# Four graph layers: the node work of layers 1, 2 and 4 is done in units of 512 nodes inside the gather passes

## The reference, cut to what matters

```python
x = _layernorm(x + GAT(x))        # 4 heads; softmax over the edges of a node; skip product; its own layer norm
x = _layernorm(x + GCN(x))        # linear, batch norm over all nodes, leaky relu, product, sum over edges, log_softmax
x = _layernorm(x + HGT(x))        # 8 heads; keys and values gathered, queries by target; product, skip, norm, elu
x = _layernorm(x + SchNet(x))     # filters from 50 edge features; sum over edges; lin2, softplus, lin
```

## Time and profile before

| what | value |
|---|---|
| runs | 9010.18 us median of 3 (9009.75 to 9013.16) |
| profiled execution | 9027.8 us, of it the span from first to last instruction 9025.8 us |
| busy | PE 5296.0, PEld 4295.5, DVE 4797.4, ACT 1743.0, POOL 6159.4 us |
| mean granted TensorE clock | 0.663 of full speed |

### The profile page before, as it was taken

How to read it: one execution, slowest core, us unless ns; L and a number is a source line. 1 busy time by engine, 2 the same in 40 slices (tenths; PEclk the granted TensorE clock), 3 DMA queues, 4 the chain that set the end, 5 groups by cost and what they waited for, 6 DMA issues and landing times. The chain is left out here.

```text
span 9025.8 us, 88124 instructions
## 1 busy us (share of the span) xinstructions
PE 5296.0 (59%) x27493; PEld 4295.5 (48%) x27493; DVE 4797.4 (53%) x10730; ACT 1743.0 (19%) x2681; POOL 6159.4 (68%) x6485
## 2 busy tenths in 40 slices
PE   4555555553244444444456666666656888887884
PEld 3454444443233333333335555555544555555553
DVE  5666666666522222222257777777775555555554
ACT  0000000001200000000030000000016555555553
POOL 5777777771177777777637777777745777777772
PEclk6666665666555555555577777777767788788786
DMA  5444333431133333333245555555522222222221
GB/s 175 112 116 112 112 111 113 115 112 26 31 79 75 75 77 75 76 76 77 60 126 163 164 164 165 163 165 162 165 85 69 73 74 74 73 73 73 74 73 34
DMA packets 391525, 906.28 MB, mean 100 GB/s; under 512 B 134486, under 2 KB 202897, under 8 KB 368209
## 3 DMA queue, kind: packets, MB, share of 16 engines
q0 software_dynamic: 232704, 538.22, 23.3%
q1 hardware_dynamic: 153458, 351.32, 12.9%
q10 hardware_dynamic: 4896, 11.01, 0.3%
HBM read 867.62 MB, written 32.45 MB: 100 GB/s over the span
## 5 line engine op out<-in xcount | busy, mean ns | idle before, releaser
L1647 POOL DMA_INDIRECT PM<-hgt_kv_table,src_idx x1616 | 1532.5, 948 | 655.7 <-issue 468.3
L634 POOL DMA_INDIRECT PM<-gat_table,src_idx x1616 | 1536.2, 951 | 546.1 <-issue 492.2
L2217 POOL DMA_INDIRECT TMP<-schnet_table,src_idx x1616 | 1538.7, 952 | 541.0 <-issue 490.0
L1178 POOL DMA_INDIRECT PM<-gcn_table,src_idx x1004 | 952.4, 949 | 306.1 <-issue 304.3
L1178 POOL DMA_INDIRECT TMP<-gcn_table,src_idx x612 | 578.9, 946 | 550.7 <-POOLq L1038 364.4
L1206 PE MATMUL ps<-TMP,PM 128*128 128x128 f32 x2008 | 516.0, 438 | 704.8 <-DMA PM<-gcn_table,src_idx 704.8
L1253 DVE TENSOR_TENSOR AC<-AC,ps 128x128 f32 x101 | 29.2, 289 | 1526.4 <-PE ps L1206 1526.4
L679 PE MATMUL ps<-PM 128*128 128x139 f32 x3232 | 779.7, 433 | 66.7 <-DVE PM L773 66.4
L1206 PEld LDWEIGHTS ps<-TMP,PM 128*128 128x128 f32 x2008 | 444.3, 326 | 766.1 <-DMA PM<-gcn_table,src_idx 627.9
L679 PEld LDWEIGHTS ps<-PM 128*128 128x128 f32 x3232 | 738.6, 326 | 73.1 <-DVE PM L773 72.7
L2244 PE MATMUL ps<-PM 128*128 128x128 f32 x3232 | 551.2, 325 | 335.4 <-issue 210.7
(11 more groups left out here) (386 smaller groups left out, 8790.3 us busy)
## 6 DMA issues: line engine op xcount, KB each, us to landing
PM<-local_dst_row SPq DMA_DIRECT2D x101, 1024.0 KB
PM<-local_dst_row SPq DMA_DIRECT2D x202, 512.0 KB, 3.9
PM<-in_attrT SPq DMA_DIRECT2D x101, 400.0 KB
xT<-in_rel_row SPq DMA_DIRECT2D x101, 384.0 KB, 4.7
PM<-gat_table,src_idx POOLq DMA_INDIRECT x1616
PM<-hgt_kv_table,src_idx POOLq DMA_INDIRECT x1616, 3.1
TMP<-schnet_table,src_idx POOLq DMA_INDIRECT x1616, 2.5
PM<-gcn_table,src_idx POOLq DMA_INDIRECT x1004, 2.5
```

The lines of the kernel that those rows point to most:

```text
L634: pool.indirect_dma_start(out=g[:, par, t, 0:TAB0], out_offset=None, in_=tab0_d, in_offset=bass.IndirectOffsetOnAxis(ap=src_idx[:, i * ROU ...
L1178: pool.indirect_dma_start(out=g[n % DEEP][:, k, :], out_offset=None, in_=tab1_d, in_offset=bass.IndirectOffsetOnAxis(ap=src_idx[:, n * KT ...
L1647: pool.indirect_dma_start(out=g[:, par, t, 0:2 * P], out_offset=None, in_=kv_d, in_offset=bass.IndirectOffsetOnAxis(ap=src_idx[:, i * ROUN ...
L2217: pool.indirect_dma_start(out=g[:, b, k, :], out_offset=None, in_=tab3_d, in_offset=bass.IndirectOffsetOnAxis(ap=src_idx[:, (i * SLOTS + b ...
```

## The change

Nodes are cut into 13 units of 512 (the last has 2 tiles of 128 instead of 4). The node work of layers 1, 2 and 4 is cut into stages (9, 8 and 8), and a unit takes one stage in each round, beginning at a round by which its nodes can get no more edges. The schedule is fixed when the program is built:

```diff
+PACE, LAG = 62, 60
+                s.link(dve.scalar_tensor_tensor(span, iota_f[:, 0:NR], -float(PACE), bounds[:, 0:NR], ALU.mult, ALU.add))
+                s.link(dve.tensor_reduce(ahead, span, AX.X, ALU.min))
+                s.link(dve.scalar_tensor_tensor(nar, ahead, -float(LAG), nar, ALU.is_ge, ALU.mult))
...
+        def first_round(u):
+            r = -(-(KT * P * (u + 1) + LAG) // PACE) + 1
+            return r if r < NR else None
+        def due(i, stages):
+            return [(u, i - first_round(u)) for u in range(GROUPS4) if first_round(u) is not None and 0 <= i - first_round(u) < stages]
+        def left_over(narrow, stages):
+            if not narrow:
+                return [(u, k) for u in range(GROUPS4) for k in range(stages)]
+            begun = [u for u in range(GROUPS4) if first_round(u) is not None]
+            rest = [(u, k) for u in begun for k in range(stages) if first_round(u) + k >= NR]
+            return rest + [(u, k) for k in range(stages) for u in range(len(begun), GROUPS4)]
```

```diff
+                    def unit(u, k):
+                        def by_tile(weights):
+                            for j, t_ in enumerate(tiles_of(u)):
+                                m = nc.tensor.matmul(unit_ps(u)[:, j, :], xT[:, t_ * P:(t_ + 1) * P], weights, start=True, stop=True)
+                            return m
+                        if k == 0:
+                            r = first_round(u)
+                            pe.wait_ge(acc_step, 2 * r + 6 if narrow and r is not None else 2 * NR + 8 if narrow else T + 8)
+                            if 0 < u < GROUPS4 - 1:
+                                pe.wait_ge(lin_kept, u)
+                            for j, t_ in enumerate(tiles_of(u)):
+                                m = nc.tensor.transpose(unit_z(u)[:, j, :], acc2[0:Z0, 1, t_ * P:(t_ + 1) * P], ident[0:Z0, 0:Z0])
+                            m.then_inc(z_t, 1)
+                        if k == 1:
+                            pe.wait_ge(z_kept, u + 1)
+                            by_tile(WA[:, 0:P]).then_inc(h_mm, 1)
+                        if k == 2:
+                            pe.wait_ge(h_read, u + 1)
+                            for j, t_ in enumerate(tiles_of(u)):
+                                m = nc.tensor.transpose(unit_ps(u)[:, j, :], acc2[:, 0, t_ * P:(t_ + 1) * P], ident[:, :])
+                            m.then_inc(sum_t, 1)
+                        if k == 3:
+                            pe.wait_ge(sum_read, u + 1)
+                            by_tile(WA[:, P:2 * P]).then_inc(skip_mm, 1)
+                        if k == 6:
+                            pe.wait_ge(end_x, tiles_of(u)[-1] + 1)
+                            for j, t_ in enumerate(tiles_of(u)):
+                                m = nc.tensor.transpose(unit_ps(u)[:, j, :], xn[:, t_, :], ident[:, :])
+                            m.then_inc(end_xt, 1)
+                        if k == 7:
+                            pe.wait_ge(end_xc, u + 1)
+                            pe.wait_ge(end_ld, 144)
+                            nc.tensor.matmul(unit_row(u), Wlin, xT[:, columns_of(u)], start=True, stop=True).then_inc(lin_mm, 1)
...
+                        if k == 0:
+                            act.wait_ge(self_in, u + 1)
+                            nc.scalar.activation(self_w[:, u % 2, :, :], self_w[:, u % 2, :, :], ACT.Exp).then_inc(self_exp, 1)
+                        if k == 3:
+                            rstd(0)
+                        if k == 4:
+                            rstd(1)
+                        if k == 5:
+                            act.wait_ge(end_scaled, u + 1)
+                            for j, t_ in enumerate(tiles_of(u)):
+                                nc.scalar.activation(xn[:, t_, :], et[:, u % 2, j, :], ACT.Identity, scale=w["rstd"][:, t_:t_ + 1],
+                                                     bias=w["shift"][:, t_:t_ + 1]).then_inc(end_x, 1)
+                        if k == 6:
+                            act.wait_ge(end_xt, u + 1)
+                            nc.scalar.copy(xT[:, columns_of(u)].rearrange("p (k f) -> p k f", f=P), unit_ps(u)).then_inc(end_xc, 1)
+                        if k == 7:
+                            act.wait_ge(lin_mm, u + 1)
+                            act.wait_ge(end_ld, 144)
+                            nc.scalar.activation(acc2[:, 0, columns_of(u)], unit_row(u), ACT.Identity, bias=blin).then_inc(lin_kept, 1)
...
+                        if k == 0:
+                            dve.wait_ge(z_t, u + 1)
+                            e.mark(dve.tensor_copy(zz, unit_z(u)))
+                            e.link(dve.tensor_tensor(sv, asd[:, at, 0:H0], asd[:, at, H0:2 * H0], ALU.add))
+                            dve.sem_inc(z_kept, 1)
+                            e.mark(dve.tensor_scalar(deg[:, at], zz[:, :, Z0 - 1], 1.0, None, ALU.add))
+                            e.link(dve.scalar_tensor_tensor(sv, sv, 0.2, sv, ALU.mult, ALU.max))
+                            e.link(dve.tensor_tensor(sv, sv, zz[:, :, H0:2 * H0], ALU.subtract))
+                            dve.sem_inc(self_in, 1)
+                        if k == 1:
+                            dve.wait_ge(self_exp, u + 1)
+                            e.link(dve.scalar_tensor_tensor(zz[:, :, 0:H0], zz[:, :, 0:H0], SM_EPS, sv, ALU.add, ALU.add))
+                            e.link(dve.reciprocal(zz[:, :, 0:H0], zz[:, :, 0:H0]))
+                            e.link(dve.tensor_tensor(sv, sv, zz[:, :, 0:H0], ALU.mult))
+                            dve.wait_ge(h_mm, u + 1)
+                            e.link(dve.tensor_tensor(t.rearrange(heads, c=C0), unit_ps(u).rearrange(heads, c=C0), over(sv, P, nt, H0, C0), ALU.mult))
+                            dve.sem_inc(h_read, 1)
+                        if k == 2:
+                            dve.wait_ge(sum_t, u + 1)
+                            e.link(dve.tensor_tensor(q.rearrange(heads, c=C0), unit_ps(u).rearrange(heads, c=C0), over(zz[:, :, 0:H0], P, nt, H0, C0), ALU.mult))
+                            dve.sem_inc(sum_read, 1)
+                            e.link(dve.tensor_tensor(t, t, q, ALU.add))
+                        if k == 3:
+                            if u == 0:
+                                dve.wait_ge(end_ld, 144)
+                                e.link(dve.tensor_tensor(bsum, rb[:, 0, :], rb[:, 1, :], ALU.add))
+                            dve.wait_ge(skip_mm, u + 1)
+                            e.link(dve.tensor_tensor(t, t, unit_ps(u), ALU.add))
+                            dve.sem_inc(skip_read, 1)
+                            e.link(dve.tensor_tensor(t, t, bsum.unsqueeze(1).to_broadcast([P, nt, P]), ALU.add))
+                            stats()
+                        if k == 4:
+                            rstd(0)
+                            newton(dve, e, w["rstd"][:, at], w["var"][:, at], w["diff"][:, at])
+                            e.link(dve.tensor_scalar(w["shift"][:, at], w["mean2"][:, at], 0.5, None, ALU.mult))
+                            for t_ in tiles_of(u):
+                                tt = et[:, u % 2, t_ % KT, :]
+                                e.mark(dve.scalar_tensor_tensor(tt, tt, w["shift"][:, t_:t_ + 1], rb[:, 2, :], ALU.subtract, ALU.mult))
+                            e.settle()
+                            for t_ in tiles_of(u):
+                                tt = et[:, u % 2, t_ % KT, :]
+                                e.mark(dve.scalar_tensor_tensor(tt, tt, w["rstd"][:, t_:t_ + 1], rb[:, 3, :], ALU.mult, ALU.add))
+                            e.settle()
+                            if u == 0:
+                                dve.wait_ge(x_ready, 16)
+                            e.link(dve.tensor_tensor(t, t, xn[:, at, :], ALU.add))
+                            stats()
+                        if k == 5:
+                            rstd(1)
+                            scale_and_shift(dve, e, w, at)
+                            dve.sem_inc(end_scaled, 1)
+                        if k == 8:
+                            dve.wait_ge(lin_kept, u + 1)
+                            lo = u * KT * P
+                            e.mark(dve.bn_stats(out=node_st[:, u, :], in_=acc2[:, 0, lo:min(lo + KT * P, N)]))
...
+                for n in range(GROUPS4 + 1):
+                    if n < GROUPS4:
+                        x1 = acc2[:, 0, columns_of(n)]
+                        dve.wait_ge(shifted, n + 1)
+                        dve.scalar_tensor_tensor(x1, x1, 0.01, x1, ALU.mult, ALU.max).then_inc(bent, 1)
+                    if n:
+                        at = nodes_of(n - 1)
+                        dve.wait_ge(row_mm, n)
+                        dve.tensor_tensor(hkeep[:, at, :], group_ps(2 + (n - 1) % 2, n - 1), over(dinv[:, at], P, at.stop - at.start, P), ALU.mult).then_inc(row_kept, 1)
```

(38 more changed lines are left out.)

922 lines of the change are left out of this document (424 added, 498 removed).

## The result

The changed kernel takes 8501.35 us, the median of 4 runs (8499.64 to 8505.35), against 9009.97 us before on the same chip: ratio 0.9436, 95% interval 0.942 to 0.9452. Forecast were 8510 us. The profiled execution has a span of 8499.8 us, 526.0 less than before.

A forecast was written before the change was run, and what follows sets the result against it. POOL's gathers bound the kernel. Span 9025.8 - 511 saved + 5 + 1 + 4 = 8525 us, plus 2.0 around it 8527; less 17.6 for the runs' median 8509, said as 8510; range 8480 to 8600 (8 in 10).

The forecast's parts named there:

- POOL is the bound, the stretches are the gain: Four gather passes make 8111 of 9025.8 us; three of five stretches without gathers shrink, saving 511 us.
- Layer 1's stretch: No gathers after layer 1: first gather at 2176 instead of 2450, saving 274 us, with 4 us for hops between engines.
- The batch statistics: After layer 1's leftover units: small instructions 2.4 and 1.4 us, ln, load and exp 2.2, from 2141 to 2147.
- The group pipe: End of layer 1: 12.5 groups of scale, relu and Wg product; entry 1.4, then 17.5, last 0.7 us.
- Layers 2 and 4: Stretches after the last additions of layers 2 and 4: only units 11 and 12 remain, saving 116 and 121 us.
- The six tiles of products: Layer 2's leftover chain: three tiles with cold PE at 2.5 us and three at 1.4, 11.6 us.
- What layer 1's pass pays: Units inside layer 1's rounds lengthen its pass by 5 us, 11 units at half a microsecond; bounds 0 and 33.
- a need of 3.7 against a slack of 3.9: Layer 1, stages 6 and 7 at a round's border: 3.7 us added, 3.9 us before POOL's next group 0; nothing stops.
- The holes of a round: Layer 1: DVE's idle 5.7 us after its scans hides a unit's stage, 6.1 us for stage 4, but for 0.4.
- Layer 4's pass: Minus ln 2 on 128x512, about 0.4 us on DVE, eleven times, holds the port shared with POOL: 4 us.
- Rival 3: DVE instructions with two SBUF inputs stop POOL for their length in layers 1, 2, 4: 138 us, 8648; 5%.
- The median of the runs: Whole kernel: the runs' median lies 17.6 us below the profiled execution, so 8527 becomes 8509, said as 8510.

The follow-up runs named there:

- the units after the rounds: Changed kernel, but all 13 units of layers 1, 2 and 4 follow the rounds, one after the other; 9278.87 us, 1.0278 of the kernel before.
- the three runs of 128x2048: Changed kernel, layer 2's one-hot with two SBUF inputs as tensor_tensor, scalar_tensor_tensor, or with a wait ahead; gathers sum to 1889, 1884, 1695 us against 1528.

## Why the prediction was right

- **POOL is the bound, the stretches are the gain.** Right, and shown by the units after the rounds.
- **Layer 1's stretch (saved 274, measured 275.3).** The chain is 0.7 us shorter than forecast. The batch statistics took 8.2 us (2143.2 to 2151.5), not 6: 2.55 us pass between the last unit and the first of them, in which DVE waits for nothing that the trace shows. The group pipe took 19.7 us, forecast 20. The last round's addition came 25.3 us after the last gather, 23.4 before, which the sum had left as it was. That the stretch comes out within 1.3 us is partly luck: the 4 us that I added for hops between engines were not needed, and they cover the 2.2 us of the statistics and the 1.9 of the addition.
- **Layers 2 and 4 (116 and 121, measured 119.0 and 121.1).** The six tiles of products, which I had at 11.6 us, took from 4222.7 to 4231.5, 8.8. A table load of 1.28 us stands between ln and exp after the change too (at 4214.27 and 8490.21), as the sums had it.
- **What layer 1's pass pays (5 us).** The sum was right, its parts were not. By layer 3's pass of the same execution layer 1's is longer by 8.4 us with the units (2027.5 - 2019.1) and by 3.7 and 4.6 without (before, and with the units after the rounds): 4 to 5 us. I had half a microsecond of stops in each unit. Only 0.8 us are stops for a unit's sums, in two units at half clock, where the need of 3.6 us passes the slack of 3.2. I had a need of 3.7 against a slack of 3.9; in the other units the need is 1.6 to 2.6. Both sizes were too large, and that their order held was luck. One stop in round 2 makes 0.7 us, and the kernel with all units after the rounds has it too (1.2). The durations of the gathers make 3.0 us; those more than 12 ns over the median sum to 7.6 us before and to 9.6 and 11.6 in the two runs after.
- **The holes of a round.** Right in the main. Ahead of the scans that follow a stage 4 DVE is idle 0.22 us in seven of eleven units (next fence) and 0.8 to 2.1 in the others, instead of 5.71; the wait at the border of stages 6 and 7 is 3.2 to 4.2 us at the full clock, 5.2 at half, forecast "about 5".

```profile
1223.67 0.87 DVE L1083 BATCH_NORM_STATS2 TMP<-TMP 128x6 f32<-128x128 f32 x4
1225.51 0.41 DVE L1008 TENSOR_TENSOR_SCAN TMP<-PM,ps 64x128 f32<-64x128 f32 x1 [0.22 <-PE ps L806]
```

- **Layer 4's pass (4 us for minus ln 2).** Too large by a factor of 20 or more. In the changed kernel's profiled execution only one of the eleven `tensor_scalar`s of 0.43 us (L2419) makes a gather late, by 0.13 us, and so it is in its second one; most of them begin 0.03 to 0.10 us after a gather has begun and end before it does, and leave it whole. Layer 4's pass says nothing on it: four executions with short gathers have 2024.5, 2028.6, 2030.0 and 2030.1, which is 5 to 11 us over layer 3's; before it was 6.2 over, and 8.8 with the units after the rounds.
- **Rival 3.** The mechanism is real, my ground for 5% was not: layer 4's median gather says nothing on a longer instruction, which the three runs of 128x2048 show. Here its price is some 2 to 4 us in layer 1 instead of 138, since the change's instructions with two SBUF inputs are 0.7 us or less and many gathers begin beside them and not inside. The Trainium skill ("SBUF — State Buffer", Who interferes with whom) states that a DVE instruction with two SBUF inputs contends with GpSimd's reads; the trace agrees in layer 2 (2.71 us for the gather that begins inside, 0.94 for the one ahead). For the two-port modes the Trainium skill (same section) states that whoever issues first gets the pair for the whole instruction. A hold for the whole instruction fits the `tensor_scalar` (the gathers that it stops end 0.12 or 0.82 us after it), if it is in such a mode, which no run shows; who began first does not decide there, as gathers that had begun up to 0.36 us ahead of it were stopped too.
- **The median of the runs.** The 17.6 us that I took off for the profiled execution are about what the longer gathers make: 4 times 1616 times 3 ns is 19 us (an estimate; the kernel before was profiled only with the longer ones). The changed kernel's profiled execution had the short ones and is at its median. So the span was forecast 25 us too long (8525 against 8499.8), some 19 of it for this.

## What to carry to other kernels

When one engine sets the pace, cut the work between its passes into stages and give each a round of its own. The same unit cost under half a microsecond spread over nine rounds, 26 us as one lump in the tightest layer, and 29 alone; a stage is free while what it adds to the tightest wait (1.6 to 2.6 us) is less than the slack there (3.2 us), and every microsecond above is paid in full. The stretch after layer 3, 181 us, is what is left of the kind; it was not tried.

Beside gathers issued by POOL keep long DVE instructions to one SBUF input, or short and apart; and a `tensor_scalar` from SBUF to SBUF is not free there either (0.56 us a round for 1.28 us), while the `tensor_tensor` with its second input in PSUM cost nothing, though it took 2.27 us.

## What the hardware showed that was not expected

- A DVE instruction with two SBUF inputs can stop a gather that begins up to 2.14 us ahead of it, while the instruction in front still runs; a wait between the two takes this away (3.6 to 1.65 us a round).
- Sixteen such instructions of 0.27 us in a row lengthened one gather from 0.94 to up to 7.18 us.
- A `tensor_scalar` of 1.28 us from SBUF to SBUF also stops gathers under way, begun up to 0.36 us ahead of it; these end 0.12 us after it, those that begin inside it 0.82 us after it.
- The gathers take 944 ns in one profiled execution and 947 in another on the same chip, in all layers alike (2 ns more in layer 3), which is 19 us of this kernel.
